# A two-layer block on one core: the second token pair's last normalisation is done by feature, after its only transposition

## What is computed

```
x = x + attn(layernorm(x))       # inside: x1 = x0 + (sigmoid(r) * wkv) @ Wo.T
                                 #         x2 = x1 + sigmoid(cr) * (silu(kk) @ Wval.T)
z = layernorm(x)                 # "the last norm": (x - mean) / sqrt(var + 1e-5), over the 512 features
g, u = split(z @ w_gate_up.T)    # 2048 gate and 2048 up columns
out = x + (silu(g) * u) @ w_down.T
```

## Time and profile before

| | |
|---|---|
| median of 3 runs | 1059.4 us (1059.13 to 1059.77) |
| the profiled execution's own time | 1059.37 us |
| its span, first to last instruction | 1057.5 us |
| busy: PE / DVE / POOL / ACT | 1049.2 / 683.8 / 589.3 / 520.5 us |
| TensorE clock granted | full, 2.4 GHz, in all 40 slices |

### The profile page before, as it was taken

The page is one execution under the profiler, slowest core; times in us unless marked ns, Lnnn a source line. Parts: engine busy times, 40 slices in busy tenths (PEclk is TensorE's granted clock), DMA queues, the critical chain, the costliest instruction groups (busy, mean ns, idle before and its releaser), DMA issues.

```text
span 1057.5 us, 13599 instructions
## 1 busy us (share of the span) xinstructions
PE 1049.2 (99%) x4738; PEld 869.1 (82%) x4738; DVE 683.8 (65%) x1212; ACT 520.5 (49%) x881; POOL 589.3 (56%) x492
## 2 busy tenths in 40 slices
PE   8999999999999999999999999999999999999998
PEld 7888888788888888888888888888888888888887
DVE  7888757786545564565459666776559566666655
ACT  7867576766444354323355433334445344444442
POOL 7776383735765545444447755564563266555552
PEclk9999999999999999999999999999999999999999
DMA  8002052277653344742323666565436445454432
GB/s 322 1 1 41 1 130 65 86 212 279 235 179 129 130 160 134 230 152 92 121 79 110 239 219 219 192 191 194 175 132 210 135 152 191 151 159 160 159 101 80
DMA packets 45236, 157.21 MB, mean 149 GB/s; under 512 B 4080, under 2 KB 4208, under 8 KB 40560
## 3 DMA queue, kind: packets, MB, share of 16 engines
q1 hardware_dynamic: 29712, 108.02, 29.4%
q0 software_dynamic: 15168, 48.24, 15.3%
q10 hardware_dynamic: 288, 0.09, 0.0%
HBM read 97.60 MB, written 58.72 MB: 148 GB/s over the span
## 4 chain that ended last, share of the span: by engine, by line
PE 92%; POOL 4%; DVE 2%; ACT 2%; issue 0%; DMA 0%; SPq 0%; ACTq 0%; DVEq 0%
PE bank L582 14%; PE bank L584 14%; PE bank L583 14%; PE bank L571 13%; PE bank L573 13%; PE bank L572 13%; PE bank L767 2%; PE bank L768 2%; PE bank L766 2%; POOL operand L1897 2%; POOL weights L1885 1%; PE bank L747 1%; ACT made L947 1%; PE bank L646 1%; POOL weights L1897 0%; PE bank L812 0%
## 5 line engine op out<-in xcount | busy, mean ns | idle before, releaser
L582 PE MATMUL bank<-combo,left 128*128 128x512 f32 x672 | 262.3, 390 | 0.4 <-DVE bank L1636 0.4
L584 PE MATMUL bank<-combo,left 128*128 128x512 f32 x672 | 261.5, 389 | 0.0
L583 PE MATMUL bank<-combo,left 128*128 128x512 f32 x672 | 261.4, 389 | 0.0
L1581 DVE TENSOR_TENSOR resid<-bank,resid 128x512 f32<-128x512 f32 x176 | 120.5, 689 | 143.3 <-PE bank L573 142.6
L1949 POOL TENSOR_TENSOR inner<-made,inner 128x512 fp32r<-128x512 f32 x96 | 125.7, 1331 | 130.1 <-ACT inner L1074 130.1
L1919 POOL TENSOR_TENSOR left<-quart,left 128x512 fp32r<-128x512 f32 x96 | 114.7, 1219 | 86.7 <-ACT left L1039 48.0
L571 PE MATMUL bank<-right,inner 128*128 128x512 f32 x384 | 149.5, 389 | 0.0
L573 PE MATMUL bank<-right,inner 128*128 128x512 f32 x384 | 149.4, 389 | 0.0
L572 PE MATMUL bank<-right,inner 128*128 128x512 f32 x384 | 149.4, 389 | 0.0
L582 PEld LDWEIGHTS bank<-combo,left 128*128 128x128 f32 x672 | 126.1, 188 | 27.4 <-DVE bank L1636 1.1
L584 PEld LDWEIGHTS bank<-combo,left 128*128 128x128 f32 x672 | 126.1, 188 | 26.1
(11 more groups left out here) (186 smaller groups left out, 1929.9 us busy)
## 6 DMA issues: line engine op xcount, KB each, us to landing
kept_left<-left SPq DMA_DIRECT2D x24, 1792.0 KB, 8.2
left<-kept_left POOLq DMA_DIRECT2D x24, 1024.0 KB, 7.1
left<-kept_left POOLq DMA_DIRECT2D x24, 768.0 KB, 4.9
quart<-wide SPq DMA_DIRECT2D x24, 512.0 KB, 4.1
tall_staged<-tall SPq DMA_DIRECT2D x48, 256.0 KB, 5.2
raw<-kept SPq DMA_DIRECT2D x32, 256.0 KB, 6.1
landed<-wts SPq DMA_DIRECT2D x20, 256.0 KB, 6.1
resid<-x POOLq DMA_DIRECT2D x4, 1024.0 KB, 9.6
```

The source lines that it names most:

```text
L582: pe.matmul(acc[:], hi, combo[:, c, k, 0, :], start=fresh and k == 0, stop=False, skip_group_check=True)
L583: pe.matmul(acc[:], hi, combo[:, c, k, 1, :], start=False, stop=False, skip_group_check=True)
L584: mm = pe.matmul(acc[:], lo, combo[:, c, k, 0, :], start=False, stop=k == 1, skip_group_check=True)
L1581: dve.tensor_tensor(tile, A[s][:], tile, ALU.add).then_inc(added, 1)
```

## The change

The second pair's x2 is transposed once, before the norm, in place in `resid`; the norm is then done by feature. A mean or scale now differs along the row and is the same in all partitions, so the 512 means and the 512 scales of a block are stored to DRAM and loaded back spread over all 128 partitions, into `extra`. Each feature tile takes two DVE instructions (subtract, multiply) where a token tile took one. The transposition of block 2 moves to unit 24 and that of block 3 to unit 28; both turns are gone. Stage 3's operands wait for `z3_ready` (DVE) and not for `t3_kept` (ACT). The last output tile is made, added and stored in two halves of 256 columns. At the start, ACT's copy of the first K weight tile stands behind three of four operand tiles, and the second V weight tile behind the receptance gate. The order of `last_norm(u, 1)` and `right_sums` in one place of DVE's `unit` is swapped. In the diff below, `keep_rows` and `load_rows` are SP's; the first `norm3` is PE's and the second ACT's; `x2_stats`, `norm3_rows` and the last piece are DVE's.

```diff
-NORM3_UNIT = tuple(piece_unit(j, NORM_PIECES - 1) + 1 for j in range(BLOCKS))
+NORM3_UNIT = tuple(piece_unit(j, NORM_PIECES - 1 if j < PAIRS else SUBS) + 1 for j in range(BLOCKS))
-TURN_UNIT = {2: 28, 3: FIRST[3] + 1}
-TURN_AFTER = {j: tiles_in(u, 1)[0] for j, u in TURN_UNIT.items()}
+PLAIN_WHOLE = PLAIN_ORDER[:-1]
+COLUMN_HALVES = (slice(0, HALF), slice(HALF, BT))
...
+        rows = nc.dram_tensor("rows", (PAIRS, 2, BT), F32, kind="Internal").ap()
...
+            def keep_rows(j):
+                sp.wait_ge(ln_rstd, 2 * BLOCKS + j)
+                for n, source in enumerate((stats2[:, :, 0], rstd2[:])):
+                    sp.dma_start(rows[j - PAIRS, n].rearrange("(s p) -> p s", p=P), source,
+                                 allow_slow_non_contiguous=True).then_inc(rows_moved, 16)
+            def load_rows(j):
+                sp.wait_ge(rows_moved, 32 * (2 * (j - PAIRS) + 1))
+                sp.wait_ge(z3_ready, SUBS * j)
+                for n in range(2):
+                    sp.dma_start(extra[:, n, :],
+                                 rows[j - PAIRS, n:n + 1, :].broadcast_to((P, BT))).then_inc(rows_moved, 16)
...
+                for j in range(PAIRS, BLOCKS):
+                    if u == NORM3_UNIT[j]:
+                        keep_rows(j)
+                        load_rows(j)
...
             def norm3(j):
-                pe.wait_ge(z3_ready, SUBS * (j + 1))
+                if j < PAIRS:
+                    pe.wait_ge(z3_ready, SUBS * (j + 1))
+                else:
+                    pe.wait_ge(x2_moments, SUBS * (j + 1))
+                source = fin[j % 2] if j < PAIRS else resid[:, j]
...
-            def turn(j):
...
-                for b, f in PLAIN_ORDER[KT:]:
+                for b, f in PLAIN_WHOLE[KT:]:
                     part_of(b, f, 0)
                     part_of(b, f, 1).then_inc(out_psum, 1)
+                b, f = PLAIN_ORDER[-1]
+                pe.wait_ge(added, TILES + 1)
+                for columns, bank in zip(COLUMN_HALVES, (A[0], B[f])):
+                    part_of(b, f, 0, columns, bank)
+                    part_of(b, f, 1, columns, bank).then_inc(out_psum, 1)
...
             def norm3(j):
                 act.wait_ge(t3_psum, SUBS * (j + 1))
+                place_of = raw[j] if j < PAIRS else resid[:, j]
...
-            matrix_hi(ITEM_K, range(1))
             act.wait_ge(const_done, 3)
-            mixed("r", 0, behind=1)
+            mixed("r", 0, behind=1, amid=lambda: matrix_hi(ITEM_K, range(1)))
...
-            matrix_hi(ITEM_V, range(2))
+            matrix_hi(ITEM_V, range(1))
             receptance_gate(0)
-            matrix_hi(ITEM_V, range(2, KT))
+            matrix_hi(ITEM_V, range(1, KT))
...
             def x2_stats(j):
-                if j:
+                if j == BLOCKS - 1:
+                    dve.wait_ge(rows_moved, 32)
+                elif j:
                     dve.wait_ge(z3_ready, SUBS * j)
...
+            def norm3_rows(j, k):
+                dve.wait_ge(t3_kept, SUBS * (j + 1))
+                dve.wait_ge(rows_moved, 64 * (j - PAIRS + 1))
+                dve.tensor_tensor(raw[j % 2][:, k, :], resid[:, j, k, :], extra[:, 0, :],
+                                  ALU.subtract).then_inc(z3_part, 1)
+                dve.wait_ge(z3_part, KT * (j - PAIRS) + k + 1)
+                dve.tensor_tensor(raw[j % 2][:, k, :], raw[j % 2][:, k, :], extra[:, 1, :],
+                                  ALU.mult).then_inc(z3_ready, 1)
...
-                                norm3(j, 2 * (piece - SUBS - 1))
-                                norm3(j, 2 * (piece - SUBS - 1) + 1)
+                                tile = norm3 if j < PAIRS else norm3_rows
+                                tile(j, 2 * (piece - SUBS - 1))
+                                tile(j, 2 * (piece - SUBS - 1) + 1)
...
+            b, f = PLAIN_ORDER[-1]
+            for n, (columns, bank) in enumerate(zip(COLUMN_HALVES, (A[0], B[f]))):
+                dve.wait_ge(out_psum, TILES + len(PLAIN_WHOLE) + n + 1)
+                tile = resid[:, 2 + b, f, columns]
+                dve.tensor_tensor(tile, bank[:, columns], tile, ALU.add).then_inc(added, 1)
```

More of the change, by code:

```diff
@@ L561, in _ @@
             load_plain()
-            for n, (b, f) in enumerate(PLAIN_ORDER):
+            for n, (b, f) in enumerate(PLAIN_WHOLE):
                 sp.wait_ge(added, TILES + n + 1)
                 sp.dma_start(out_blocks[2 + b][:, f, :], resid[:, 2 + b, f, :]).then_inc(out_stored, 16)
-            sp.wait_ge(out_stored, 16 * (2 + 2 * KT))
+            b, f = PLAIN_ORDER[-1]
+            for n, columns in enumerate(COLUMN_HALVES):
+                sp.wait_ge(added, TILES + len(PLAIN_WHOLE) + n + 1)
+                sp.dma_start(out_blocks[2 + b][:, f, columns], resid[:, 2 + b, f, columns]).then_inc(out_stored, 16)
+            sp.wait_ge(out_stored, 16 * (2 + 2 * KT + 1))
         @block.tensor
@@ L746, in norm3 @@
                     for k in range(KT):
-                        mm = pe.transpose(A[s][:, k * P:(k + 1) * P], fin[j % 2][:, s, k * P:(k + 1) * P], ident[:])
+                        mm = pe.transpose(A[s][:, k * P:(k + 1) * P], source[:, s, k * P:(k + 1) * P], ident[:])
                     mm.then_inc(t3_psum, 1)
-            def turn(j):
[L752 to L758, removed]
             def side_product(acc, q, a, c, fresh):
@@ L802, in plain_tiles, with part_of @@
             def plain_tiles():
-                def part_of(b, f, i):
+                def part_of(b, f, i, columns=slice(0, BT), bank=None):
                     c = PLAIN_MADE[2 * i + b]
@@ L808, in part_of @@
                     pe.wait_ge(down_lo, 2 * GROUPS + i + 1)
-                    acc = (A, B)[b][f]
+                    acc = (bank or (A, B)[b][f])[:, columns]
                     hi, lo = (plain_right[:, i, part, f * P:(f + 1) * P] for part in range(2))
[L811 to L814, removed]
+                    x_hi, x_lo = (side_at(KEY_UNITS - 1, c, part)[:, columns] for part in range(2))
+                    pe.matmul(acc, hi, x_hi, start=i == 0, stop=False, skip_group_check=True)
+                    pe.matmul(acc, hi, x_lo, start=False, stop=False, skip_group_check=True)
+                    return pe.matmul(acc, lo, x_hi, start=False, stop=i == 1, skip_group_check=True)
                 first = [f for b, f in PLAIN_ORDER if b == 0]
@@ L870, in unit @@
                         norm3(j)
-                for j in TURN_UNIT:
-                    if u == TURN_UNIT[j]:
-                        turn(j)
                 if q > 0:
@@ L1138, in plain_right_hi @@
                     act.activation(plain_right[:, i, 0, :], plain_staged[:, i, :], ACT.Copy).then_inc(down_hi, 1)
-            def turn(j):
-                act.wait_ge(turn_psum, SUBS * (j - 1))
-                for n in range(TURN_AFTER[j], TURN_AFTER[j] + SUBS):
-                    s = n % SUBS
-                    act.activation(resid[:, j, :, s * P:(s + 1) * P], A[s][:].rearrange("p (k t) -> p k t", k=KT),
-                                   ACT.Copy).then_inc(turned, 1)
             def gated_hi(u):
@@ L1156, in norm3 @@
                 act.wait_ge(t3_psum, SUBS * (j + 1))
+                place_of = raw[j] if j < PAIRS else resid[:, j]
                 for n in range(NORM3_AFTER[j], NORM3_AFTER[j] + SUBS):
                     s = n % SUBS
-                    act.activation(raw[j % 2][:, :, s * P:(s + 1) * P], A[s][:].rearrange("p (k t) -> p k t", k=KT),
+                    act.activation(place_of[:, :, s * P:(s + 1) * P], A[s][:].rearrange("p (k t) -> p k t", k=KT),
                                    ACT.Copy).then_inc(t3_kept, 1)
@@ L1687, in add_x @@
                 dve.wait_ge(o2, q + 1)
-                dve.wait_ge(turned, 2 * SUBS)
+                dve.wait_ge(t3_kept, SUBS * BLOCKS)
                 side_add(OX, 0, q % 2, ox_added)
```

15 lines of the change are left out of this document (8 added, 7 removed).

## The result

The changed kernel takes **1068.8 us** (median of 6 runs, 1065.08 to 1069.91), the kernel before 1059.2 beside it (6 runs, 1059.03 to 1059.77): a ratio of 1.0082, mean to mean, with an interval of 1.007 to 1.0094. It is slower, and the forecast of 1056.0 with its range to 1058.4 was wrong. They leave the 3.7 us between it and the median unexplained; what the record shows of them stands under "What stays open".

The account below looks back on a forecast made before the run. PE was taken as the bound, busy 1049.2 of 1057.5 us. From 1059.37, -3.50 (turns) +0.30 (norm tiles) +0 (DRAM) -0.20 (last tile) +0 (start) = -3.40 gave 1055.97, forecast 1056.0, range 1055.2 to 1058.4 with rivals.

Parts of the forecast that it names:

- The two turns, -3.50: On PE, the transposition turns of blocks 2 and 3 disappear, saving 1.75 and 1.74 us.
- Eight norm tiles on DVE, +0.3: Four DVE pieces, units 24, 25, 28, 29, each grow by 1.75 us; +0.3 us, from 0 to +2.9.
- sum_v's 0.78: Unit 25: sum_v's margin before PE wants it, 1.31 us less 0.53 of delay, leaves 0.78.
- one meeting's 1.10: A two-input DVE instruction beside POOL's work takes 1.51 us instead of 0.41, costing 1.10.
- The means and scales go through DRAM, 0 us: Two transfers in sequence on SP were taken as hidden by the rest of unit 24: 0 us, up to several.
- 12.6 us: Time for both transfers, from SP's issue at 688.62 to DVE's need for the rows at 701.25.
- rival 2: Rows come late in units 24 and 28, DVE then PE stand 4.8 us a block: 1065.3 us; chance 0.05.
- The last tile, -0.2: At the end, halving the last tile shortens DVE's sum and the store: -0.2 us, from -0.5 to +1.1.
- the estimate beside it: Last tile's twelve 256-column matmuls at 0.109 us each by the skill's page, 1.31 us in all.
- The start, 0: At the start, two weight tiles copied later by ACT cost 0 us, from -0.2 to +0.2.

Follow-up runs that it names:

- kernel without rows: The changed kernel without the transfers of means and scales and DVE's waits for them; DVE reads whatever lies in extra: 1055.66 us, ratio 0.9962.
- the tail alone: The kernel before with the last output tile in halves and nothing else: 1059.21 us, ratio 0.9995.
- The delay made by DVE: The kernel without rows, with 7 (block 2) and 5 (block 3) extra DVE instructions ahead of the norm piece: 1064.61 us, ratio 1.0042.
- the packed form: The changed kernel with means and scales packed in one tile, stored in 128 pieces of 32 bytes, read by DVE with strides: 1062.88 us, ratio 1.0029.
- block 2 later: The changed kernel with block 2's last two norm pieces one unit later, block 3's not moved: 1059.59 us, ratio 0.9997.
- ACT's queue: The changed kernel with the 4-byte stores of means and scales issued by ACT instead of SP: 1066.93 us, ratio 1.0072.

## Why the prediction was wrong

**The two turns, -3.50: right.** They are gone, and the 16 transpositions of units 24 and 28 let PE go on at once, as forecast. The kernel without rows gained 3.7 us with the tail's part in it.

**Eight norm tiles on DVE, +0.3: mechanism right, size 0.** In the kernel without rows the instructions and distances are the predicted ones, and in unit 25 the x2 sum met POOL once. The working took sum_v's 0.78 for the tight place, and less one meeting's 1.10 it let 0.32 reach PE. But the weight sums behind the seed met POOL for less: 0.97 and 0.95 us, where 1.51 and 0.95 stood before. The seed had 0.40 us of margin and sum_v 0.71, so one meeting fitted, and nothing reached PE.

**The means and scales go through DRAM, 0 us: this is the step that failed.** It said "two transfers in sequence" have 12.6 us and "two at 6 still fit". Measured in block 2: 15.2 us from the second store's issue, and 16.4 from the first, which stands where the 12.6 were counted from. The first hop was mis-sized. I priced a 2 KB transfer by its bytes, between a 256 KB transfer alone and one in a full queue, although the prediction itself noted that its pieces are of 4 bytes and that the trace has no such row. It took 9.2 and 11.3 us, more than the upper bound; the second hop took 3.4 to 5.6, inside its bounds. A bound taken from the nearest rows is none when those rows differ in the very thing that is new. What the Trainium skill says on its page "DMA: Bandwidth & Descriptors", section "Specifications", that pieces below 512 bytes are read, modified and written, spoke against the change and had only the chance of rival 2. By that rule alone 4 and 16 bytes would fare alike; the runs part them, 7.9 to 11.3 us against 3.9 to 5.1.

**Rival 2 was the case**, at 0.05, and its time of 1065.3 is near the profiled 1065.08, though 3.5 us under the median. In parts it was right by cancellation, which is luck: it had 4.8 us a block from two hops of 9.1; in fact the hops, landing to landing, were 9.2 and 6.0 in block 2, 11.3 and 5.8 in block 3, and the lateness of 3.93 and 3.04 us became 9.9 us of PE time by what the rival left out: the POOL meetings that a late piece runs into (1.8 us in unit 25; in unit 29 four instructions took 5.79 where 4 x 0.69 = 2.76 is their own time) and 1.5 us at the lower clock. Its argument against itself, that two `fin` loads in the queue are fewer than four, did not matter: with wide pieces the same queue delivered in 3.9 to 5.1 us.

**The last tile, -0.2: right in direction, -0.48 in the profile.** The twelve matmuls start 0.120 us apart, as taken, and not 0.109 as in the estimate beside it, and the sum takes 0.42. The rest is the store: the last half landed 1.7 us after its issue, the last whole tile before 2.0, so 0.3 and not 0.05. In the times of the tail alone the gain isn't resolved. **The start, 0: right.**

**What stays open.** *Why a store of 512 pieces lands so late.* In block 2 the 4-byte packets are recorded until 693.4, and the landings follow at 696.47 and 699.00; in block 3 until 759.1, with landings at 764.88 and 766.93. In between the DMA engines show next to nothing (a share of 0.00 from 694 to 699, of 0.03 from 759.5 to 764.8). With 16-byte pieces the packets are recorded until 694.4, and both stores had landed by 694.98. So the time goes by behind the recorded packets; what passes in it no trace shows.

*Why the other executions of the changed kernel took up to 4.8 us more than the profiled one.* No trace of a longer one was taken, but the mean granted clock of each is on record. For 1065.08, 1065.89, 1067.97, 1069.67 and twice 1069.91 us it is 0.998, 0.998, 0.995, 0.994 and twice 0.993: the longer the execution, the lower the clock. A shortfall of 0.002 of the span is 2.1 us of full-speed time, one of 0.007 is 7.5; the difference of 5.4 is, within the rounding, the size of the 4.8. So the longer executions fit longer stretches at the 1.2 GHz level. The delay made by DVE shows that such a stretch can differ (5.15 us against 3.08) behind nearly the same wait (5.19 against 5.31). Whether the landings were later as well isn't shown.

## What to carry to other kernels

Price a small transfer by its pieces, not its bytes: 2 KB in 4-byte pieces landed later than 256 KB loads around it. If per-token numbers must get into another layout, turning them on PE first (0.11 us) and storing whole rows was the cheaper road here (1056.36 us against 1062.88 for the packed form). A new wait on an engine that has under 1 us to spare is a place where both ends must be known before its cost is called zero, and the work behind that wait must be laid against what the other engines do at its new time.

## What the runs showed that was not expected

- Landing of a 2 KB store: 7.9 to 11.3 us in 512 pieces of 4 bytes on SP's queue, 8.3 to 12.7 on ACT's, 3.9 to 5.1 in 128 pieces of 16 bytes; a 4 KB store 4.2 to 5.8 in 128 pieces of 32 bytes, at most 3.7 and 1.5 in 8 pieces of 512 bytes.
- The slow stores and others in flight go together: the store of `left` issued at 751.04, ahead of block 3's rows, landed after 14.8 us, in the packed kernel after 8.2 and before the change after 8.0. Which of the two holds up the other isn't shown.
- The clock fell to the 1.2 GHz level behind PE's waits of 5.31, 5.19 and 3.01 us, but also behind one of 2.19 (block 2 later, granted 0.60 in the 2.8 us from 772.70 on) and one of 2.26 (packed rows, granted 0.51 in the 3.4 us from 712.80 on). It did not fall behind waits of 2.64 (the change), 2.94 (ACT's queue) and 3.34 (packed rows, unit 26; granted 1.00 in the 3.5 us from 731.70 on). The length of a gap alone doesn't tell it here.
